# Layer 0 attention: six score steps of eight have their maxima subtracted by VectorE, two by TensorE

## What is computed

```
q = jnp.einsum('bsm,hmd->bhsd', x, kernel[0])
k = jnp.einsum('bsm,hmd->bhsd', x, kernel[1])
v = jnp.einsum('bsm,hmd->bhsd', x, kernel[2])
scale = jnp.float32(1.0 / (d * d * h))
scores = jnp.einsum('bhsd,bhtd->bhst', q, k) * scale
attn = jax.nn.softmax(scores, axis=-1)
out = jnp.einsum('bhst,bhtd->bhsd', attn, v)
```

## Time and profile before

| | |
|---|---|
| median of 3 runs | 2895.15 us (2895.09 to 2895.74) |
| the profiled execution | 2896.77 us, of which the span is 2895.0 us |
| PE busy | 2721.0 us, 94% of the span |
| DVE busy | 2446.9 us, 85% |
| POOL busy | 2476.9 us, 86% |
| ACT busy | 1580.6 us, 55% |
| mean granted TensorE clock | 0.973 |
| attention of layer 0 | from about 195 us (first look) to about 1380 us |

### The profile page before, as it was taken

One profiled execution on the slowest core, in us unless ns is written; L12 is line 12 of the kernel. 1 busy time (PEld: TensorE's weight loads), 2 busy tenths in 40 slices (PEclk: granted clock), 3 DMA queues, 4 the chain that ended last, 5 costly groups with the idle time before them and its releaser, 6 DMA issues. The chain is left out here.

```text
span 2895.0 us, 46572 instructions
## 1 busy us (share of the span) xinstructions
PE 2721.0 (94%) x17528; PEld 1131.5 (39%) x17528; DVE 2446.9 (85%) x3303; ACT 1580.6 (55%) x1974; POOL 2476.9 (86%) x1190
## 2 busy tenths in 40 slices
PE   4989999999999999998589599999999999999996
PEld 3433333433333333343365133333333333333333
DVE  6678888888888888885578699999999999999994
ACT  4345555555555555555255355555555556555654
POOL 0229999999999999999245599999999999999997
PEclk9999999999999999999699699999999999999998
DMA  4441111111111111100334412211111222122200
GB/s 115 149 146 30 30 30 30 30 30 30 30 30 30 30 28 28 27 9 1 89 106 145 140 58 58 54 49 32 41 58 58 58 58 58 58 58 58 58 1 15
DMA packets 68881, 155.28 MB, mean 54 GB/s; under 512 B 20514, under 2 KB 34219, under 8 KB 66483
## 3 DMA queue, kind: packets, MB, share of 16 engines
q1 hardware_dynamic: 67634, 150.21, 18.7%
q0 software_dynamic: 1024, 2.10, 0.3%
HBM read 113.34 MB, written 38.93 MB: 53 GB/s over the span
## 5 line engine op out<-in xcount | busy, mean ns | idle before, releaser
L933 POOL TENSOR_TENSOR a_sums<-a_sums,room 128x1024 f32<-128x1024 f32 x512 | 1196.0, 2364 | 9.4 <-ACT room L759 6.0
L680 PE MATMUL a_ov<-room,va 128*64 128x512 f32 x4096 | 991.5, 605 | 0.0
L759 ACT ACTIVATE room<-room,sscale 128x1024 f32<-128x1024 f32 x512 | 588.5, 1150 | 491.7 <-DVE room L858 491.7
L825 DVE TENSOR_REDUCE a_mx<-a_jb 128x1 f32<-128x1024 f32 x496 | 606.8, 1223 | 183.1 <-PE a_jb L636 180.8
L933 POOL TENSOR_TENSOR a_sums<-room 128x1024 f32<-128x1024 f32 x256 | 604.1, 2361 | 72.8 <-ACT room L763 44.8
L820 DVE CUSTOM_DVE_ANT_0 a_junk<-a_jb,a_tab 128x1024 bf16<-128x1024 f32 x501 | 609.8, 1217 | 48.7 <-DVE a_m L831 36.3
L858 DVE TENSOR_TENSOR room<-a_st,a_tab 128x1024 f32<-128x1024 f32 x512 | 624.2, 1220 | 14.2 <-PE a_st L669 12.9
L763 ACT ACTIVATE room<-room,sscale 128x1024 f32<-128x1024 f32 x256 | 294.0, 1148 | 351.5 <-DVE room L845 351.5
L635 PE MATMUL a_jb<-a_kh,a_qh 64*128 64x512 f16 x997 | 384.8, 386 | 16.1 <-DVE a_mx L820 3.3
L669 PE MATMUL a_st<-a_qh,a_kh 64*128 64x512 f16 x2048 | 390.4, 378 | 0.1
L680 PEld LDWEIGHTS a_ov<-room,va 128*64 128x64 f32 x4096 | 248.5, 136 | 362.1 <-issue 296.3
(11 more groups left out here) (237 smaller groups left out, 2500.6 us busy)
## 6 DMA issues: line engine op xcount, KB each, us to landing
a_tab<-bias_line SPq DMA_DIRECT2D x16, 1984.0 KB, 10.6
qk_high<-room SPq DMA_DIRECT2D x16, 512.0 KB, 2.6
qk_low<-room SPq DMA_DIRECT2D x16, 512.0 KB, 3.6
a_qh<-qk_high SPq DMA_DIRECT2D x32, 256.0 KB, 4.2
a_kh<-qk_high SPq DMA_DIRECT2D x32, 256.0 KB, 4.8
a_ql<-qk_low SPq DMA_DIRECT2D x32, 256.0 KB, 6.5
a_kl<-qk_low SPq DMA_DIRECT2D x32, 256.0 KB, 7.1
qk_high<-er_split SPq DMA_DIRECT2D x32, 256.0 KB, 2.1
```

Of the source, the lines that this page charges most:

```text
L680: last = nc.tensor.matmul(ov[t * DH:(t + 1) * DH, :], k.va[:, 2 * s + t, h * DH:(h + 1) * DH], prob[:, step % RING, t * QC:(t + 1) * QC], ...
L759: nc.scalar.activation(prob[:, r, :], prob[:, r, :], ACT.Exp, scale=k.sscale[:, layer:layer + 1])\
L825: nc.vector.reduce_max(mx[:, j // 2, j % 2:j % 2 + 1], scratch(n, j), AX.X).then_inc(max_done, 1)
L933: nc.gpsimd.tensor_tensor(a, first, prob[:, step % RING, :], ALU.add).then_inc(summed, 1)
```

## The change

`by_row` becomes true in layer 0 for steps 0 and 4 alone. Steps 2 and 6 of each chunk lose their fourth round and get a `subtract_maxima`. The counts on the semaphore `lowered` follow, and TensorE, before it writes a slot of `st`, now waits for whichever engine read the step that was in it, two steps before.

```diff
         def by_row(step):
-            return bias or step % 2 == 0
+            return bias or step % 4 == 0
+
+        def lowered_by(step):
+            return 3 * (step // 4) + step % 4
...
-                if step >= 2 and by_row(step):
+                if step >= 2 and by_row(step - 2):
                     pe.wait_ge(st_read, step - 1)
                 elif step >= 2:
-                    pe.wait_ge(lowered, step // 2)
+                    pe.wait_ge(lowered, lowered_by(step - 2))
...
                 elif not by_row(step):
-                    act.wait_ge(lowered, step // 2 + 1)
+                    act.wait_ge(lowered, lowered_by(step))
```

## The result

| | before | changed |
|---|---|---|
| median | 2895.12 us (2894.77 to 2895.74, 4 runs) | 2947.16 us (2946.50 to 2948.33, 4 runs) |
| span of the profiled execution | 2895.0 us | 2944.8 us |

The ratio is 1.0177 with a 95% interval of 1.0164 to 1.0190: 52 us more, where 2946 was forecast and 2931 to 2970 given as the range. The first instruction behind the attention of layer 0, VectorE's product with the gate, starts at 1379.80 before and at 1428.99 in the changed kernel: 49.2 us of it are in this stage.

The account below looks back on a forecast made before the run. PE and DVE were taken as balanced by the 1.71 us `jb` round trip; +0.82 us in each of 62 chunks (+50.8) plus small end terms gave +51 on 2895.15, so 2946 us, range 2931 to 2970.

Parts of the forecast that it names:

- The rounds' price: Two PE rounds fewer per layer-0 chunk, steps 2 and 6: at most 0.03 to 0.07 us gained of each 0.217.
- The subtractions' price: Two more DVE subtractions per layer-0 chunk, after the maxima of steps 2 and 6: 1.13 us each, 2.26 in all.
- The chain: Links of maxima, looks, subtractions and `values` that set one layer-0 chunk: 19.14 us, against 18.32 before.
- The table's starts: Forecast start times of looks, maxima, subtractions and `values` in one layer-0 chunk, counted from PE's first look at 0.
- The sum: Layer-0 attention: +0.82 us in each of 62 looking-ahead chunks, +50.8, with the ends +51 us, total 2946.
- The two end terms: Ends of layer-0 attention: first chunk grows 0.4 us less than the others; the last two chunks add 0.4.
- PE's time: Rival: PE's busy time bounds layer-0 attention, so 0.43 us less a chunk gives -27 us, 2868; chance 0.04.
- Cancelling: Rival: DVE's idle pieces and PE's saved 0.43 absorb the subtractions; 18.3 us a chunk, 2895; chance 0.02.
- Full durations: Rival: DVE's instructions cost full row lengths or a look slips; chunk 19.94 us, +100 us, 2995; chance 0.05.
- Another engine as the limit: POOL in layer-0 attention: needs 17.72 us a chunk and keeps up; no chance given.
- The clock: Rival: PE's short stops lower its granted clock to a mean of 0.9; 19.6 us a chunk, 2975; chance 0.04.
- the walk: One layer-0 chunk worked through by start times, each engine in its order: 18.32 us before, 19.14 after; chance 0.85.

Follow-up runs that it names:

- Experiment 1: Kernel before, layer 0: TensorE's fourth round left out in steps 2 and 6, no subtraction in its place; 2894.86 us, ratio 0.9999.
- experiment 2: Changed kernel with the fourth round kept in steps 2 and 6 too, so their maxima are taken off twice; 2947.03 us, ratio 1.0178.
- experiment 7: Changed kernel with rounds in steps 0, 2 and 7 and five subtractions, in steps 1, 3, 4, 5, 6; 2888.17 us, ratio 0.9976.
- experiment 4: Changed kernel with rounds in steps 0 and 7; row ahead of pair (2,3)'s second look, one `values` step between later pairs' score steps; 2895.68 us, ratio 1.0003.
- experiment 3: Changed kernel with its two rounds a chunk in steps 0 and 7 instead of 0 and 4, still six subtractions; 2905.84 us, ratio 1.0037.
- experiment 5: Changed kernel with TensorE's round kept in step 6, only step 2 given to VectorE, five subtractions; 2912.99 us, ratio 1.0060.
- experiment 6: Changed kernel with TensorE's round kept in step 2, only step 6 given to VectorE, five subtractions; 2929.01 us, ratio 1.0117.
- experiment 8: Kernel before with the row's four matmuls moved ahead of the second look in pair (2,3) of layer 0; 2902.55 us, ratio 1.0025.

## Why the prediction was right

- *What bounds it.* The profile's page says PE, 94% busy; the prediction said that PE and DVE are in step by the one `jb`. Experiment 1 shows it: 0.43 us less work a chunk on the engine that is "99.9% busy", and the chunk went from 18.32 to 18.31. One reading on the way was loose: the 262 waits of the earlier trace rows are those of the weight loads, which run ahead of the matmuls. The matmuls themselves stood at two places a chunk, the 0.19 and 0.04 that the prediction names.
- *The rounds' price*, forecast at 0.03 to 0.07 each at most: the two together brought 0.01 with DVE as before, and nothing with DVE late (experiment 2).
- *The subtractions' price*, 1.13 each from start to start: 716.89 to 718.02 in the changed kernel. They don't add up to 2.26 a chunk, since 1.44 of it falls into time in which DVE idled: 3.35 us before, 1.91 now.
- *The chain*: 19.14 forecast, 19.14 measured, and the waits of TensorE 0.73 and 0.26 for 0.75 and 0.28. The table's starts hold to 0.02 us.
- *The sum*: 62 x 0.82 and the ends gave +51; the stage grew by 49.2 in the profiles, and the medians moved by 52. From the first merge of the stage to the last, 62 chunks, it is 1137.4 before (194.69 to 1332.10) and 1187.4 in the changed kernel (193.91 to 1381.26): +49.9. The two end terms were each wrong and cancelled: the first chunk grew by 0.81 (19.40 to 20.21) and not by 0.4 less than the others, and from the last merge to the product with the gate it is 47.70 before and 47.73 now, not 0.4 more. That forecast and median agree to 1 us is partly luck, since single executions of one kernel differ by more.
- *The rivals.* PE's time: experiments 1 and 2. Cancelling: out by the result. Full durations: the chunk isn't 19.94. Another engine as the limit: experiment 7. The clock: the granted clock was 1.00 in the stretch in which PE was busy 287.3 of 300 us, as in the row with short stops. By the Trainium skill (TensorE: Matmul & The Clock Gate, A second HAM failure mode: psum-queue depth-cycling) brief stops can bring the clock down; no run here shows that, with stops up to 0.74 us.
- *Small misses.* DVE's busy share was forecast as some 95% and is 91%: the walk's own 17.23 of 19.14 is 90%, so the 95% didn't follow from it. DVE's idle time before the change lay before six of the eight maxima, in pieces of up to 0.8 us from start to start, not before each one and up to 0.7. And the walk was right for the order of matmuls that it was taken from; on another order (experiment 4) it was 0.5 us a chunk too short.

The walk gave the chunk of seven kernels (the changed one, experiments 1 to 3 and 5 to 7) to within 0.05 us, all in TensorE's old order, and failed for the two in a new one (experiments 4 and 8), of whose transitions it had no row.

## What to carry to other kernels

When two engines hand a single buffer back and forth, work out the round trip from the rows (here 0.43 + 1.28 us) and lay it beside the work that each engine has between two hand-overs. An engine that seems busy all the time can then have slack, and taking work off it brings nothing, while work given to the other side costs what its place in the chain says: the same count of instructions cost 52 us or 11 depending on the step. Write one period of both queues down by start times and try the placements there first; and measure before trusting it for an order whose transitions no row shows.

## What the runs showed of the hardware that I had not expected

- TensorE going from matmuls on 64 of its rows to matmuls on all 128 cost about 0.1 us here: the round before is 0.31 long from start to start instead of 0.22 in experiments 4 and 8. A block of `values` adds about 0.15 to its matmuls (1.87 for the eight of a pair, 1.01 for the four of one step). Four such changes and blocks a chunk are already in the kernel before, by these figures about a microsecond of 18.3 (an estimate).
- VectorE's rows overlap: 1.22 us long and 1.14 apart, through seven instructions in a row in the changed kernel (713.49 to 720.28, six pitches of 1.13). The Trainium skill (VectorE: DVE Perf Modes, The DRAIN you can't avoid) has the next operation wait for an empty pipe, unless it is one that is not held; the end in a row here is later than the point from which the next may start, so sums over a chain must be made from starts.
